# Two transformer blocks in float32 on one core: at each row's seam, three parts of the next row's value projection are issued ahead of the transposes of the normalised row

## The reference

```
x = layernorm(x + attention0(x))   # rmsnorm, 16 heads of 64, softmax over 256 keys, output projection
x = layernorm(x + moe0(x))         # 8 experts (128 -> 256 -> 128, gelu) weighted by the top 2 gates, and a shared expert
x = layernorm(x + attention1(x))   # per token: 16 heads of 8 attend to each other, projection
x = layernorm(x + moe1(x))         # 8 experts (128 -> 512 -> 128, gelu), top 2 gates
```

## Time and profile before

| | |
|---|---|
| median of three timed executions | 1562.2 us |
| the profiled execution | 1567.07 us |
| its span in the trace | 1565.3 us |
| mean granted PE clock, as a share of 2.4 GHz | 0.976 |
| busy: ACT, POOL | 860.9 us (55%), 514.5 us (33%) |

### The profile page before, as it was taken

How to read it: one execution, slowest core, us unless ns; L and a number is a source line. 1 busy time by engine, 2 the same in 40 slices (tenths; PEclk the granted TensorE clock), 3 DMA queues, 4 the chain that set the end, 5 groups by cost and what they waited for, 6 DMA issues and landing times.

```text
span 1565.3 us, 34497 instructions
## 1 busy us (share of the span) xinstructions
PE 1421.9 (91%) x12096; PEld 1249.4 (80%) x12096; DVE 985.5 (63%) x2534; ACT 860.9 (55%) x2361; POOL 514.5 (33%) x415
## 2 busy tenths in 40 slices
PE   6897999999999999999999999999999999998847
PEld 5675888888888888878888888888888887887747
DVE  4456576675757667575666757667575766757482
ACT  5564655656465564647556464655646465463403
POOL 3206061340605134060522506043250614315040
PEclk9898999999999999999999999999999999998978
DMA  7000000000000000000000000000000000000000
GB/s 239 4 2 1 5 2 8 0 7 0 0 7 0 7 0 7 0 0 7 0 7 0 7 0 0 7 0 7 0 1 5 0 7 0 3 1 1 4 1 7
DMA packets 14088, 13.78 MB, mean 9 GB/s; under 512 B 1625, under 2 KB 12770, under 8 KB 13794
## 3 DMA queue, kind: packets, MB, share of 16 engines
q1 hardware_dynamic: 14050, 13.27, 2.6%
HBM read 11.17 MB, written 2.10 MB: 8 GB/s over the span
## 4 chain that ended last, share of the span: by engine, by line
issue 62%; POOL 17%; POOLq 14%; PE 4%; DVE 1%; ACT 1%; DMA 0%; DVEq 0%; SPq 0%
POOLq L329 8%; POOL hid L466 6%; POOL hid L471 6%; POOLq L473 5%; POOL std_inv L427 2%; PE bank_F L1101 1%; POOL up_lo L436 1%; POOL x L488 1%; POOL x_plus L450 1%; POOL rms_inv L443 1%; PE bank_S L983 0%; DMA b_out<-in_b_out 0%; ACT probs L544 0%; DVE hid L743 0%; DVE hid L761 0%
## 5 line engine op out<-in xcount | busy, mean ns | idle before, releaser
L1101 PE MATMUL bank_F<-down,hid 128*128 128x128 f32 x3072 | 374.9, 278 | 34.6 <-DVE x L731 34.0
L1101 PEld LDWEIGHTS bank_F<-down,hid 128*128 128x128 f32 x3072 | 359.4, 193 | 46.3 <-DVE x L731 38.1
L544 ACT ACTIVATE probs<-bank_S,neg_max 128x256 f32<-128x256 f32 x512 | 235.5, 475 | 179.0 <-DVE neg_max L652 178.9
L652 DVE TENSOR_REDUCE neg_max<-bank_S 128x2 f32<-128x512 f32 x256 | 164.6, 684 | 83.5 <-PE bank_S L983 80.2
L471 POOL TENSOR_TENSOR hid<-hid,qkv 128x1024 f32<-128x1024 f32 x62 | 177.1, 2857 | 47.1 <-ACT hid L560 47.1
L731 DVE SCALAR_TENSOR_TENSOR x<-bank_F,gates,x 128x128 f32<-128x128 f32 x512 | 155.2, 345 | 31.6 <-PE bank_F L1101 21.4
L523 ACT ACTIVATE probsT<-bank_T 128x512 f32<-128x512 f32 x256 | 139.6, 605 | 44.1 <-PE bank_T L1012 44.0
L426 POOL TENSOR_TENSOR var_eps<-mv,ln_eps 128x2 f32<-128x2 f32 x64 | 12.5, 195 | 428.5 <-DVE mv L690 428.5
L441 POOL TENSOR_TENSOR mean_sq<-sum_sq,one_over_d 128x2 f32<-128x2 f32 x16 | 3.1, 194 | 455.1 <-ACT h_row L518 455.1
L1012 PE MATMUL bank_T<-ident,probs 128*128 128x128 f32 x1024 | 138.4, 279 | 0.1
L459 POOL TENSOR_TENSOR hid<-qkv 128x1024 f32<-128x1024 f32 x47 | 112.2, 2386 | 66.6 <-ACT qkv L523 66.6
(11 more groups left out here) (167 smaller groups left out, 3259.1 us busy)
## 6 DMA issues: line engine op xcount, KB each, us to landing
x_row<-in_x SPq DMA_DIRECT2D x16, 128.0 KB, 2.1
down<-in_w SPq DMA_DIRECT2D x1, 2048.0 KB, 14.0
out<-x SPq DMA_DIRECT2D x16, 128.0 KB, 1.8
hid<-in_w SPq DMA_DIRECT2D x1, 1536.0 KB, 7.8
hid<-in_rw SPq DMA_DIRECT2D x1, 1024.0 KB, 6.6
hid<-in_wv SPq DMA_DIRECT2D x1, 512.0 KB, 3.8
hid<-in_wq SPq DMA_DIRECT2D x1, 512.0 KB, 4.7
hid<-in_wk SPq DMA_DIRECT2D x1, 512.0 KB, 5.6
```

The source lines that it names most:

```text
L544: ins = sc.activation(probs[:, h // 2 % 2, h % 2, t, :], unit.bank(f"S{h}")[:, t * S:(t + 1) * S], ACT.Exp, bias=neg_max[:, h, t:t + 1], a ...
L652: ve.tensor_reduce(neg_max[:, h, :], v.bank(f"S{h}")[:, :].rearrange("p (t k) -> p t k", t=NT), AX.X, ALU.max, negate=True).then_inc(max_r ...
L1101: ins = te.matmul(bank[:, (j * NT + t) * P:(j * NT + t + 1) * P], hid[:, e, k, tokens(t)], down[:, e, k, :], start=k == 0, stop=k == m - 1)
```

## The change

One line moves down by two places in `pe_units`:

```diff
     put("F", "D1e6", "D1e7", on=c)
     put("A", "V0", on=nxt)
-    put("A", "X1T", on=a)
     put("G", "V1", on=nxt)
     put("A", "V2", on=nxt)
+    put("A", "X1T", on=a)
     put("G", "U0_0", "U0_1", on=a)
     put("A", "R0", on=a)
```

## The result

The changed kernel is slower. In the first comparison its median is 1568.76 us (14 executions) against 1563.4 us for the kernel before (14 executions): ratio 1.0028, 95% interval 1.002 to 1.0036. Two later comparisons gave 1.0016 (1.0007 to 1.0025) and 1.0013 (1.0004 to 1.0022). The three average 1.0019, about 3 us. (The quotient of the first comparison's two medians, 1.0034, lies inside its interval.) Two single executions, of 7531 us for the kernel before and of 4994 us for filler_behind, are left out of every ratio. The forecast was 1.8 us faster, 1560.4 us with a range of 1557.2 to 1564.3.

What follows compares the result with a forecast made beforehand. The prediction took the chain norm (DVE), transposes (PE), split (DVE) to set the start of the experts, with PE dense from there. Terms 1.3 + 0.5 + 0 = 1.8 us gave 1562.2 - 1.8 = 1560.4 us, range 1557.2 to 1564.3.

Steps and rivals of the forecast that it cites:

- The thirteen loop iterations, 13 x 0: Loop seam: V1 and V2 fit the hole before the transposes, U0_0 starts as before; nothing won.
- Iteration 0, 1.3 us won: First seam: V1 and V2 fill the hole, the clock stays whole, U0_0 starts earlier; 1.3 us won, bounds 0.7 to 1.45.
- Iteration 1, 0.5 us won: Second seam: U0_0 starts 1.3 us earlier but half clock is expected again; 0.5 us won, bounds 0 and 2.2.
- Sum: All seams together: 1.3 + 0.5 + 0 = 1.8 us faster.
- Rival C: Idle PE before U0_0 lowers the clock in each loop iteration: 22 us slower, 1584 us; mild form 1564.3 us; chance 0.08.
- What I carried over: Whole kernel: the timed runs' median of 1562.2 us taken as the base from which 1.8 us was subtracted.
- A: Iteration 1 keeps its clock (2.2 us), iteration 0 gives 1.4, the loop 1.3: 1557.3 us; chance 0.24.
- B: Early gain eaten by iteration 1's lost gain and a later half-clock stretch, or no effect: 1562.2 us; chance 0.18.

Runs made afterwards that it cites:

- filler_behind: Moved order in iterations 0 and 1 only, plus six unused matmuls behind the transposes there; ratio 0.9991 to the kernel before.
- copies_late: Moved order in the 13 loop iterations only, with ScalarE's copies of V1 and V2 held until the transposes are filled; no ratio, loop iteration 92.201 us.
- before_again: The kernel before, run once more with no edit; ratio 1.0003 to the kernel before.
- written_only: Moved order in iterations 0 and 1 only, the loop keeping the order of the kernel before; ratio 1.0018 to it.
- it0_only: Moved order in iteration 0 only, everything else as in the kernel before; ratio 1.0004 to it.
- it1_only: Moved order in iteration 1 only, everything else as in the kernel before; ratio 1.0008 to it.
- loop_filler: Order of the kernel before, plus six filler matmuls between V0 and the transposes in the 13 loop iterations; no ratio, loop iteration 92.204 us.
- after_again: The changed kernel as it is, second comparison; ratio 1.0016 to the kernel before.
- after_third: The changed kernel as it is, third comparison; ratio 1.0013 to the kernel before.
- loop_only: Moved order in the 13 loop iterations only, the rest as in the kernel before; ratio 0.9996 to it.
- warm_moved_again: Repeat run: moved order in iterations 0 and 1, plus 2 and 4 filler groups behind V2 ahead of the transposes; ratio 0.9986 to the kernel before.

## Why the prediction was wrong

- **The thirteen loop iterations, 13 x 0.** Nearly right, with a small term missing. The timing was as worked out: V1 and V2 fit, the wait for V0's bank cost nothing, U0_0 1.72 us behind the transposes. I let "DVE and POOL issue the same work in the same order" stand for the same durations; PE's matmuls beside the product cost it 0.06 us. The four traces of the loop in the moved order other than copies_late average 92.199 us (92.190 to 92.215). Five traces with the old order there and no filler anywhere (before, before_again, written_only, it0_only, it1_only) average 92.146, and with the five that have filler in iterations 0 and 1 alone 92.150 (92.127 to 92.172): 13 x 0.05 = 0.7 us. The norm's end hangs on POOL, as I wrote, but POOL's end hangs a little on PE. The claim that ACT's moved copies touch nothing held as far as loop_filler shows, where the product takes 2.88 us without them; only I looked at the copies and not at the matmuls.
- **Iteration 0, 1.3 us won.** This step failed in its second half. That U0_0 comes 5.6 us behind V0 instead of 7.0 to 7.15 was right in all five traces without filler (where the old order has a whole clock there, in copies_late, it is 5.77 and next to nothing is won). "I take it that the clock then stays whole" counted PE's activity ahead of the transposes and not behind them. In the first trace of the changed kernel it held, which was luck. In four of the five traces with the moved order there the clock fell over U0 (for 6.8 us in after_again, after_third and written_only, for 3.4 in it0_only), and the five average (72.88 + 75.96 + 75.95 + 75.99 + 74.22) / 5 = 75.0 us from V0 to V0, against 74.7 for the six of the old order without filler at this seam (before, before_again, loop_only, it1_only, copies_late, loop_filler). Won: nothing, if not -0.3 us.
- **Iteration 1, 0.5 us won.** This is the step that turned the sign. "If the clock comes back one stretch later than now ... nothing is left" named the event, but as a lower bound and not as the likely case, and priced it too low. By its own terms the case was worth 0.65 - 1.7 = -1.05 us and not nothing, so the bound of 0 was a slip of the sum. I named the hole ahead of the transposes, but put at nothing what V1 and V2 did behind the transposes while the clock was low: with them PE was busy for 3.26 us of a stretch's first 3.4 (it0_only), without them for 2.20 (it1_only). The stretch is 10.2 us in all five traces. From V0 to iteration 2 the moved order takes 102.03, 101.70, 101.71, 101.65 and 102.04, on average 101.8 us, and the six old ones 100.36, 100.34, 99.63, 99.57, 100.67 and 99.66, on average 100.0: 1.8 us lost. My sum compared only the two stretches that I had in one trace; in half of the old order's traces the clock came back after 3.4 us, with V1 and V2 running in that stretch, and I had taken 6.8 as given. Against the old order with 3.4 us the moved order loses 2.0 to 2.5 us, and against the one with 6.8 us 1.0 to 1.7.
- **Sum.** 0.7 + 0.3 + 1.8 = 2.8 us, 0.18%, against 0.13 to 0.28% measured. That leaves no large term out, though each term is an average of few traces. What remains of the first comparison's 0.28% can't be placed: the start (up to V0 of iteration 0, 65.0 to 67.7 us) and the end (121 to 126 us behind iteration 15's transposes) differ by more from trace to trace than is sought.
- **Rival C** had the mechanism, PE's idle time before U0_0, and the wrong place. In the loop the clock stayed at 1.00 in every trace, as I argued from the old hole. I should have asked the question of the two seams where a long hole already was. The rule of the Trainium skill beside it ("TensorE: Matmul & The Clock Gate", the section on oscillation in real kernels), on kernels whose waits throttle PE in each pass of a loop, did not apply to this loop: no trace shows the clock below 1.00 in it, 1286.6 us in the windows of the changed kernel, with holes of 0.23 and 1.29 us in each pass. That the sum would be C's "by that rule" was more than the section says, since its kernels wait longer in each pass than this one.
- **What I carried over**: "1562.2 - 1.8", a median of three executions. Fourteen gave 1563.4, and the kernel before had medians up to 1566.1 in the later comparisons. The forecast time was off by that also.
- **Rivals A and B**: A, in which iteration 1 keeps its whole clock, didn't happen: its stretch grew. B's half, that the early gain is eaten, is what occurred in iteration 0.

## What to carry to other kernels

Work that stands between two dependent steps of another engine is not only cover for a wait. Here it was also PE's activity while the clock was low behind a long hole: with it there the clock was back after 3.4 or 6.8 us, without it after 10.2. And it could run slowly without being missed. Before moving such work into an earlier hole, look for what is left between the holes. One hole of 1.55 us in each pass of the loop was free here. Two of 1.8 and 1.1 us around 0.4 us of transposes were followed by a stretch at half clock in four of five traces (6.8 us long in three), and two of 1.1 and 1.2 us in one of two. Where a long wait can't be avoided, harmless matmuls into a free bank, ended before the wait does, were worth more than either order (0.3%, ten groups of three in the whole kernel).

And a share of a per cent needs more than one trace: compare distances between the same instructions, seam by seam, over several executions, and not spans.

## What the runs showed of the hardware

- A granted clock that is whole at the transposes can fall 0.5 to 0.7 us after dense work has begun again (73.0 against U0_0 at 72.35 in after_third; 147.6 against 147.06 in warm_moved_again). In the 3.4 us before, PE had been busy for 1.06 and 1.04 us; the 6.8 us at half clock that followed were solidly busy (6.80 of 6.80).
- With the fall at the same point of iteration 1, the clock came back after 3.4 us where PE was busy for 3.26 of them (it0_only) and after 10.2 us where it was busy for 2.20 of the first 3.4 (it1_only).
- Matmuls on TensorE lengthened a GpSimd product of 128 x 1024 float32 running beside them from 2.82 to 2.88 us, with nothing else moved (before and loop_filler).
- With the clock whole, the distance from iteration 1's U0_0 to iteration 2's transposes is 90.3 to 90.4 us. In the old order it is the same with a low stretch of 3.4 us, which V1 and V2 fill (90.39 to 90.46), and 91.1 to 91.5 with one of 6.8 us. In the moved order it is 93.4 with 6.8 us, all of it on U0 and what follows, and 93.7 to 94.1 with 10.2 us, of which 7.5 to 8.4 us lie there.
